# One-hot rows of a graph kernel: fifty operations with a scalar key per partition in place of six on pairs of keys

## The reference

```python
msg = jnp.concatenate([x_i, x_j, ea2], axis=1) @ W + b
agg = jax.ops.segment_sum(msg, dst2, num_segments=n)
...
x = _layernorm(x + log_softmax(layer2(relu(layer1(x)))), axis=-1)
```

## Time and profile before

| what | value |
|---|---|
| median of 3 runs | 245.8 us (245.77 to 246.25) |
| the profiled execution | 245.65 us |
| its span in the profile | 243.9 us |
| mean granted clock of TensorE | 0.976 |
| busy: PE, DVE, ACT, POOL | 199.1, 176.6, 115.2, 159.9 us |
| DVE operations in the whole profile | 438, of which 150 make one-hots |

### The profile page before, as it was taken

One profiled execution on the slowest core, in us unless ns is written; L12 is line 12 of the kernel. 1 busy time (PEld: TensorE's weight loads), 2 busy tenths in 40 slices (PEclk: granted clock), 3 DMA queues, 4 the chain that ended last, 5 costly groups with the idle time before them and its releaser, 6 DMA issues.

```text
span 243.9 us, 5544 instructions
## 1 busy us (share of the span) xinstructions
PE 199.1 (82%) x2089; PEld 180.9 (74%) x2089; DVE 176.6 (72%) x438; ACT 115.2 (47%) x235; POOL 159.9 (66%) x336
## 2 busy tenths in 40 slices
PE   1001665999989999899998999989999999999930
PEld 0000564998878889789887898878979999999930
DVE  4059999898768997689976897768201293999881
ACT  2023462677757767577675776757720010111110
POOL 6758887299999999999999999999663000000000
PEclk9999995899999999999999999999999999999996
DMA  2542220000000000000000000000000001011000
GB/s 53 124 126 74 73 36 5 3 1 3 2 3 0 3 0 4 0 3 4 1 3 0 3 0 1 4 0 5 0 3 3 0 3 31 3 31 25 18 16 20
DMA packets 12579, 4.18 MB, mean 17 GB/s; under 512 B 11911, under 2 KB 12126, under 8 KB 12551
## 3 DMA queue, kind: packets, MB, share of 16 engines
q1 hardware_dynamic: 10711, 1.77, 4.1%
q0 software_dynamic: 1840, 2.04, 3.4%
HBM read 2.98 MB, written 0.81 MB: 16 GB/s over the span
## 4 chain that ended last, share of the span: by engine, by line
PE 43%; POOL 35%; DVE 10%; DMA 5%; issue 3%; ACT 1%; POOLq 0%; ACTq 0%; DVEq 0%
PE pset L831 21%; PE acc L823 10%; PE pset L798 5%; DMA adj<-in_dst,adj 5%; POOL u L371 4%; POOL deg L370 4%; POOL t L383 3%; POOL t L387 3%; POOL u L374 3%; POOL z L382 3%; POOL zr L385 3%; POOL base L393 2%; POOL z L391 2%; POOL z L389 2%; DVE ohr L497 2%
## 5 line engine op out<-in xcount | busy, mean ns | idle before, releaser
L712 ACT ACTIVATE adj<-pset 125x1000 bf16<-125x1000 f32 x75 | 77.4, 1032 | 10.0 <-PE pset L798 9.1
L823 PE MATMUL acc<-x,adj 125*125 125x195 bf16 x625 | 73.6, 255 | 0.0
L497 DVE TENSOR_TENSOR ohl<-iota,keyl 128x1000 bf16<-128x1000 bf16 (+1 forms) x75 | 56.6, 755 | 12.1 <-PE dense L811 12.1
L798 PE MATMUL pset<-ohr,ohl 128*125 128x125 bf16 x600 | 58.6, 251 | 3.8 <-DVE ohr L497 3.8
L823 PEld LDWEIGHTS acc<-x,adj 125*125 125x125 bf16 x625 | 57.8, 139 | 3.2
L497 DVE TENSOR_TENSOR ohr<-iota,keyr 128x1000 bf16<-128x1000 bf16 (+1 forms) x75 | 57.1, 762 | 0.0
L798 PEld LDWEIGHTS pset<-ohr,ohl 128*125 128x125 bf16 x600 | 49.6, 151 | 5.5 <-DVE ohr L497 4.0
L831 PE MATMUL pset<-z,adj 125*125 125x192 bf16 x625 | 52.8, 246 | 0.0
L831 PEld LDWEIGHTS pset<-z,adj 125*125 125x125 bf16 x625 | 51.7, 136 | 0.3
L526 DVE TENSOR_REDUCE s_sum<-acc 125x65 f32<-125x195 f32 x25 | 9.1, 363 | 18.4 <-PE acc L823 18.0
L748 ACT ACTIVATE x<-x 125x192 f32<-125x192 f32 (+2 forms) x6 | 2.6, 426 | 38.5 <-DVE x L583 38.5
(11 more groups left out here) (114 smaller groups left out, 269.5 us busy)
## 6 DMA issues: line engine op xcount, KB each, us to landing
x_nat<-in_x SPq DMA_DIRECT2D x1, 781.2 KB
out<-x SPq DMA_DIRECT2D x2, 187.5 KB
out<-x SPq DMA_DIRECT2D x3, 93.8 KB
out<-x SPq DMA_DIRECT2D x1, 125.0 KB
adj<-in_dst,adj POOLq DMA_INDIRECT x5, 5.6
adj<-in_edges,adj POOLq DMA_INDIRECT x5, 4.2
adj<-in_edge_attr,adj POOLq DMA_INDIRECT x5, 4.5
se_scratch<-adj SPq DMA_DIRECT2D x5, 2.4 KB
```

What stands on the lines that cost most here:

```text
L497: ins = dve.tensor_tensor(out=oh[s][:, :, :, :], in0=iota2[:, 0:Q, :].unsqueeze(1).broadcast_to([128, n, Q, 2]), in1=key[:, g, k0:k0 + 2 * ...
L712: act.activation(adj4[0:Q, g, :, w0:w0 + 8 * WD].rearrange("p h (b e) -> p b h e", b=2), pset[s][0:Q, :, 0:4 * WD * G].rearrange("p b (h e ...
L798: ins = pe.matmul(pset[s][0:Q, i // 4, 0:4 * WD * G].rearrange("p (h e) -> p h e", h=G)[:, :, i % 4 * WD:(i % 4 + 1) * WD], ohl[s][:, i // ...
L823: ins = pe.matmul(acc[0:Q, 0:XW], adj4[0:Q, g, h, :], x3[:, h, :], start=(h == 0), stop=(h == G - 1))
```

## The change

`iota` holds each number once; `keyl` and `keyr` become fp32, lie in the memory of `z3` (whose part of group d is written after the keys of group d have been used), and have no padding column. For each window and each side one tensor_scalar compares `iota[:, 0:126]` with one key column, read as a scalar per partition. A one-hot row has 126 elements of which the matmul reads 125, now next to each other. Set 0 takes 18 operations, sets 1 and 2 take 16 each: 50 per group in place of 6. Two memsets of the padding go away, and the copy of the keys is one ScalarE operation per side in place of two.

```diff
-SETS = ((0, 8, 0), (9, 8, 10), (17, 8, 18))
+SETS = ((0, 8), (9, 8), (17, 8))
-        iota2 = sb("iota2", [128, SLOTS, 2], BF16)
+        iota = sb("iota", [128, SLOTS], BF16)
-        keyl = sb("keyl", [128, G, KW], BF16)
-        keyr = sb("keyr", [128, G, KW], BF16)
-        ohl = [sb(f"ohl{s}", [128, 5 if s == 0 else 4, Q, 2], BF16) for s in range(3)]
-        ohr = [sb(f"ohr{s}", [128, 5 if s == 0 else 4, G * WD, 2], BF16) for s in range(3)]
+        ohl = [sb(f"ohl{s}", [128, 9 if s == 0 else 8, Q + 1], BF16) for s in range(3)]
+        ohr = [sb(f"ohr{s}", [128, 9 if s == 0 else 8, G * WD + 1], BF16) for s in range(3)]
...
+        z3_all = sb("z3", [128, G, PW], BF16)
+        z3 = z3_all[0:Q, :, :]
+        keys_in_z3 = z3_all[:, :, :].rearrange("p g c -> p (g c)").bitcast(FP32).rearrange("p (g c) -> p g c", g=G)
+        keyl = keys_in_z3[:, :, 0:KW]
+        keyr = keys_in_z3[:, :, KW:2 * KW]
...
-            gp.iota(iota2[:, :, :], [[1, SLOTS], [0, 2]], base=0, channel_multiplier=0,
+            gp.iota(iota[:, :], [[1, SLOTS]], base=0, channel_multiplier=0,
                     allow_small_or_imprecise_dtypes=True).then_inc(consts, 1)
-            gp.memset(keyl[:, :, SINGLE + 1:SINGLE + 2], 0.0).then_inc(consts, 1)
-            gp.memset(keyr[:, :, SINGLE + 1:SINGLE + 2], 0.0).then_inc(consts, 1)
...
-                w0, n, k0 = SETS[s]
-                n = n // 2 + (s == 0)
+                w0, n = SETS[s]
+                n += s == 0
...
-                for oh, key in ((ohl, keyl), (ohr, keyr)):
-                    ins = dve.tensor_tensor(
-                        out=oh[s][:, :, :, :],
-                        in0=iota2[:, 0:Q, :].unsqueeze(1).broadcast_to([128, n, Q, 2]),
-                        in1=key[:, g, k0:k0 + 2 * n].rearrange("p (q o k) -> p q o k", o=1, k=2)
-                        .broadcast_to([128, n, Q, 2]),
-                        op=ALU.is_equal)
+                for i in range(n):
+                    for oh, key in ((ohl, keyl), (ohr, keyr)):
+                        ins = dve.tensor_scalar(oh[s][:, i, :], iota[:, 0:Q + 1], key[:, g, w0 + i:w0 + i + 1], None,
+                                                ALU.is_equal)
                 ins.then_inc(oh_ready[s], 1)
...
-                act.activation(key[:, g0:g0 + n, 0:9], src[:, :, 0:9], ACT.Copy)
-                return act.activation(key[:, g0:g0 + n, 10:26], src[:, :, 9:25], ACT.Copy)
+                return act.activation(key[:, g0:g0 + n, :], src[:, :, :], ACT.Copy)
...
-                        ohl[s][:, i // 2, :, i % 2], ohr[s][:, i // 2, :, i % 2], start=True, stop=True)
+                        ohl[s][:, i, 0:Q], ohr[s][:, i, 0:Q], start=True, stop=True)
```

More of the change, by code:

```diff
@@ L37 @@
 XW = 3 * XC
-SETS = ((0, 8, 0), (9, 8, 10), (17, 8, 18))
+SETS = ((0, 8), (9, 8), (17, 8))
 SINGLE = 8
-KW = 26
+KW = 25
 KB = 12
@@ L127, in gnn @@
         assert free[0] // (G * Q) > 5 and sums_group > 5 * (J - 1) + 2
-        keyl = sb("keyl", [128, G, KW], BF16)
-        keyr = sb("keyr", [128, G, KW], BF16)
-        ohl = [sb(f"ohl{s}", [128, 5 if s == 0 else 4, Q, 2], BF16) for s in range(3)]
-        ohr = [sb(f"ohr{s}", [128, 5 if s == 0 else 4, G * WD, 2], BF16) for s in range(3)]
+        ohl = [sb(f"ohl{s}", [128, 9 if s == 0 else 8, Q + 1], BF16) for s in range(3)]
+        ohr = [sb(f"ohr{s}", [128, 9 if s == 0 else 8, G * WD + 1], BF16) for s in range(3)]
         x3_flat = sb("x3", [Q, G * XW + 1], BF16)
         x3 = x3_flat[:, 0:G * XW].rearrange("p (g c) -> p g c", g=G)
-        z3 = sb("z3", [Q, G, PW], BF16)
+        z3_all = sb("z3", [128, G, PW], BF16)
[3 more added lines that the diff above has]
+        keyr = keys_in_z3[:, :, KW:2 * KW]
         s_sum = sb("s_sum", [Q, XC], FP32)
@@ L510, in _ @@
             dve.tensor_tensor(x3[:, :, 2 * XC:2 * XC + C], x_rest, x3[:, :, XC:XC + C], ALU.subtract).then_inc(xs_ready, 1)
-            dve.wait_ge(consts, 11)
+            dve.wait_ge(consts, 9)
             dve.wait_ge(keys_ready, 1)
@@ L810, in build_single @@
                     pe.wait_ge(keys_ready, 3 if g == 2 else 1)
-                pe.matmul(dense[0:Q, 0:G * WD], ohl[0][:, 4, :, 0], ohr[0][:, 4, :, 0], start=True, stop=True)\
+                pe.matmul(dense[0:Q, 0:G * WD], ohl[0][:, SINGLE, 0:Q], ohr[0][:, SINGLE, 0:Q], start=True, stop=True)\
                   .then_inc(built[3], 1)
```

## The result

The changed kernel takes **336.4 us** (median of 4 runs, 335.8 to 338.0), the kernel before in the same rounds 245.8 us: a ratio of 1.369 with a 95% interval of 1.364 to 1.374, so 37% slower. Its profiled execution took 335.8 us for a span of 334.0 us. The forecast was 343 us (300 to 386).

The account below looks back on a forecast made before the run. POOL bounds the loop before, VectorE after: start 23.9, one-hots 201.3, keys 5.4, attribute sums 5.3, reductions 6.4, lines 534 to 537 1.0, meetings 28, tail 70.2 give span 341.5; 1.75 more makes 343 us (300 to 386).

Parts of the forecast that it names:

- The forecast case: Main case: in the loop VectorE becomes the bound, never stopping from first one-hot to last; 343 us, chance 0.58.
- One new operation, 0.161 us: One-hot operation on VectorE: 0.073 fixed, 0.033 elements, 0.055 scalar; 1250 of them 201.3 us.
- The fourfold rate: Elements of a new VectorE one-hot operation: 0.26 ns each, 0.033 us for 126 (bounds 0 and 0.066).
- two halvings: VectorE element time: one tensor in place of two halves it, bf16 in place of fp32 halves it; 0.26 ns per element.
- the scalar price: Scalar per partition in each VectorE one-hot operation: 0.055 us, not hidden by neighbours (bounds 0 and 0.058).
- Meetings with POOL, 28 us: In 23 loop groups, each of eleven POOL operations meets a one-hot and costs VectorE 0.11 us: 28 us (0 to 66).
- The start, -0.7 us: Before the first one-hot: the halved iota lets VectorE's first cast end 0.7 us earlier, so one-hots start at 23.9 us.
- Keys, attribute sums, reductions, lines 534 to 537: VectorE's other work between first and last one-hot: 5.4, 5.3, 6.4 and 1.0 us.
- The tail, 70.2 us: Behind the last one-hots, from the build of (24, 2) to the end: all TensorE's and unchanged, 70.2 us.
- TensorE's clock: In the loop, a fall to 1.2 GHz could cost 0 to 15 us in all; taken as 0.
- the whole-instruction exclusion: Rival at one-hots beside POOL: VectorE waits a whole POOL step, 0.26 us per meeting, 66 us; 381 us, chance 0.12.
- The "faster" rival: In the loop, operations up to 0.100 us, meetings included, let VectorE keep up and TensorE's 5.55 us bind: 241.5 us, chance 0.07.

Follow-up runs that it names:

- The immediate: The changed kernel with a constant in place of the key column as scalar of each one-hot operation: 273.95 us.
- the two-row kernels: The changed kernel with one operation of 252 elements for two rows, 26 operations per group in place of 50: 252.9 us.
- the remedy worth 1.8%: The kernel before with its one-hot operations cut in two from group 3 on: 241.47 us, ratio 0.982.

## Why the prediction was right

The forecast case came true: VectorE became the bound from its first one-hot to its last, and the time is the sum over its operations. The steps one by one:

- **One new operation, 0.161 us.** Measured 0.163: 0.071 fixed, 0.060 scalar, 0.032 elements, against 0.073, 0.055 and 0.033. 1250 of them are 203.8 us, 2.5 more than forecast. The fourfold rate, which no row of before showed, was rightly read from two halvings; the scalar price was rightly read from lines 466 and 534. The immediate and the two-row kernels are what show the split. Three small misses (-0.002, +0.005, -0.001) partly cancel in it.
- **Meetings with POOL, 28 us.** This term was mis-sized: 17.6 us. The step that failed is "while DVE makes one-hots all the time, each meets one", at 0.11 each. Each does meet one, but only POOL operations with two tile inputs cost DVE anything to speak of (0.06 to 0.14 us), and four of the eleven are not of that kind. The 0.11 us itself was near the mean of the two-input ones, 0.10.
- **The start, -0.7 us.** Wrong: the first one-hot starts at 25.00 us in place of 24.64. The iota fell even more than forecast, to 0.24 us from 1.53, and VectorE's cast beside it to 0.52 from 1.42, but the gather behind takes the gain back, and the second gather's wait is 0.2 us longer. Forecast 23.9, so +1.1.
- **Keys, attribute sums, reductions, lines 534 to 537.** 5.4 + 5.3 + 6.4 + 1.0 forecast, 4.6 + 5.3 + 6.2 + 1.1 measured. The 5.4 us of before held meetings of their own: POOL's lines 356 to 360 ran beside the keys, from 34.90 to 38.18 us. In the kernel after they run beside one-hots and are 1.1 of the 17.6 us.
- **The tail, 70.2 us.** The build of (24, 2) starts at 263.78 us, and 334.0 - 263.78 = 70.2. Exact. The 0.2 us from the last one-hot (263.56 us) to that build were left out of the sum.

The differences sum to +2.5 - 10.4 + 1.1 - 0.8 - 0.2 + 0.1 + 0.2 = -7.5 us, and the span is 334.0 us in place of 341.5. So the 343 us are near 336.4 because one term was 10 us too large and the others nearly right. TensorE's clock cost nothing, as forecast: VectorE waits before none of the reductions of the loop until its last one-hot. The clock was granted at 0.88 in the loop in place of 1.00, a mean of stretches at the two levels, 1.2 and 2.4 GHz, in a loop in which TensorE's waits for VectorE's reductions last up to 2.6 us. It waited 70 us for VectorE in all.

Of the rivals, the whole-instruction exclusion did not come true for the one-hots, either way round. POOL's 317 ns beside one-hots are its 0.31 us without them, and VectorE lost 0.07 us per POOL operation on average, not 0.26. So the rule of the Trainium skill's "SBUF — State Buffer", section "Who interferes with whom", that VectorE in a two-port mode and GpSimd fully block each other for a whole instruction, is not what these operations show. Two other pairs of this case do behave so: POOL's line 387 lasts 0.75 us beside a long two-input operation of before, to just behind that operation's end, and VectorE's first cast lasts 1.42 us beside the iota of 1.53 and 0.52 beside the one of 0.24. The "faster" rival was further off than its 0.07 said: it needed 0.100 us with the meetings, and an immediate key alone already costs 0.103.

## What to carry to other kernels

Before a few long VectorE operations are exchanged for many short ones at a faster rate, count the starts: here 0.131 of 0.163 us per operation are fixed part and scalar, and one-hots at twice the rate per element (0.25 for 0.52 ns) came to twice the work for the engine (8.15 for 3.8 us a group). What two rows per operation bring (83 us) is a measure of that. And read a loop's period group by group rather than as a mean: POOL held two groups of five, and the remedy worth 1.8% was to make the operations it waits for shorter, as long as VectorE had time to spare and no gather was being issued beside them.

## What was not expected of the hardware

- A scalar per partition costs VectorE 0.060 us in each operation, back to back, not hidden (0.163 against 0.103 us).
- An operation of 125 bf16 elements is as fast as one of 126 (0.163 us both).
- What VectorE loses to a POOL operation of the same 125 x 64 tile depends on which it is: 0.10 us beside an add of two tiles, 0.02 beside a cast to bf16. POOL loses nothing to the short one-input operations (0.318 us beside them, 0.31 without), and some 0.4 us to the long two-input ones (0.75 us).
- An iota of 128 x 256 in a pattern with a repeat took 1.53 us, one of 128 x 128 without it 0.24. Which of size and pattern does it, no run tells.
- One gather was issued in 6.75 in place of 1.73 us and one in 2.74 in place of 1.21, in the kernel whose one-hot operations of groups 0 and 1 are cut in two. The rows are of one profile; the cause is open.
